# Decoder layer on Trainium2: keys leave PSUM once as f32, and VectorE splits them from SBUF

## What is computed

```python
q = _qdq(x) @ _qdq(wq).T + bq
kv = cond @ wkv.T + bkv
k, v = jnp.split(kv, 2, axis=-1)
...
attn = jax.nn.softmax(jnp.einsum('bnhd,bmhd->bhnm', q, k) * scale, axis=-1)
o = jnp.einsum('bhnm,bmhd->bnhd', attn, v).reshape(B, N, C)
```

## Time and profile before

| what | value |
|---|---|
| runs | 1098.65, 1102.31, 1105.90 us; median 1102.31 |
| profiled execution | 1098.97 us, its span 1097.1 us |
| TensorE busy, whole span | 901.5 us (82%) |
| VectorE busy | 637.3 us (58%) |
| ScalarE busy | 442.1 us (40%) |
| GpSimd busy | 232.9 us (21%) |
| TensorE busy from 410 to 510 us | 89.0 of 100 us, granted clock 0.98 |
| VectorE, ScalarE, GpSimd in the same stretch | 69.3, 49.9, 23.7 us |

### The profile page before, as it was taken

One profiled execution on the slowest core, in us unless ns is written; L12 is line 12 of the kernel. 1 busy time (PEld: TensorE's weight loads), 2 busy tenths in 40 slices (PEclk: granted clock), 3 DMA queues, 4 the chain that ended last, 5 costly groups with the idle time before them and its releaser, 6 DMA issues.

```text
span 1097.1 us, 29125 instructions
## 1 busy us (share of the span) xinstructions
PE 901.5 (82%) x11868; PEld 687.0 (63%) x11869; DVE 637.3 (58%) x1132; ACT 442.1 (40%) x934; POOL 232.9 (21%) x200
## 2 busy tenths in 40 slices
PE   5669988997999899899989988998985059999970
PEld 3547766775777667667766776677763026666750
DVE  5557656765867586767667666866664212323225
ACT  2235444553455454445545554545453012222210
POOL 5123123112212131321123122213000510000016
PEclk9989999998999999999999999999898579999995
DMA  6634342443443343424434343434213783333323
GB/s 208 215 95 129 104 127 82 124 118 90 119 123 107 113 123 100 133 82 118 124 99 120 119 131 91 120 96 128 85 50 142 295 319 121 105 124 110 115 72 100
DMA packets 87696, 136.54 MB, mean 124 GB/s; under 512 B 11522, under 2 KB 75010, under 8 KB 85536
## 3 DMA queue, kind: packets, MB, share of 16 engines
q1 hardware_dynamic: 85040, 123.34, 36.5%
q0 software_dynamic: 2544, 11.54, 2.9%
HBM read 101.66 MB, written 33.10 MB: 123 GB/s over the span
## 4 chain that ended last, share of the span: by engine, by line
PE 53%; issue 13%; DVE 11%; DMA 10%; ACT 7%; POOL 3%; SPq 2%; DVEq 0%; ACTq 0%; POOLq 0%
PE ps L1226 10%; PE ps L1219 8%; PE ps L1506 7%; PE ps L1488 6%; PE ps L1238 5%; DMA k_dram<-k_two 4%; PE ps L1263 4%; ACT k_two L1047 4%; PE ps L1192 4%; DVE k_two L408 3%; DMA k_st<-k_dram 2%; PE ps L1283 2%; ACT pT L1073 2%; PE ps L1303 2%; PE ps L1292 2%
## 5 line engine op out<-in xcount | busy, mean ns | idle before, releaser
L414 DVE TENSOR_REDUCE negmax<-ps 112x1 f32<-112x1500 f32 x128 | 219.9, 1718 | 77.6 <-PE ps L1238 77.5
L1073 ACT ACTIVATE pT<-ps 125x448 f32<-125x448 f32 x384 | 195.0, 542 | 169.1 <-PE ps L1263 168.9
L917 POOL TENSOR_TENSOR ctx_lo<-ctx_raw,ctx_hi 128x1000 fp32r<-128x1000 f32 x47 | 109.1, 2321 | 234.0 <-DVE ctx_hi L400 232.7
L408 DVE SCALAR_TENSOR_TENSOR k_two<-ps,bk_sb,k_two 128x500 f16<-128x500 f32 x96 | 70.7, 736 | 120.1 <-ACT k_two L1047 120.0
L1263 PE MATMUL ps<-qbd,k_st 98*128 98x112 f16 x1536 | 121.7, 216 | 8.5 <-issue 4.0
L1263 PEld LDWEIGHTS ps<-qbd,k_st 98*128 98x128 f16 x1536 | 88.8, 100 | 63.3 <-issue 38.3
L1238 PE MATMUL ps<-k_st,qbd 96*112 96x500 f16 x384 | 108.1, 390 | 15.1 <-DMA k_st<-k_dram 15.1
L1047 ACT ACTIVATE k_two<-ps,bk_sb 128x500 f16<-128x500 f32 x96 | 65.1, 678 | 120.2 <-PE ps L1219 120.2
L1226 PE MATMUL ps<-wkv_hi,ctx_hi 128*125 128x256 f32 x384 | 85.5, 304 | 24.0 <-DVE k_two L408 23.7
L1283 PE MATMUL ps<-pT,v_sb 125*17 125x56 f32 x6144 | 101.4, 215 | 0.5 <-issue 0.5
L1031 ACT COPY v_sb<-ps 125x512 f32<-125x512 f32 x96 | 56.4, 587 | 85.2 <-PE ps L1226 85.2
(11 more groups left out here) (197 smaller groups left out, 1278.4 us busy)
## 6 DMA issues: line engine op xcount, KB each, us to landing
k_st<-k_dram SPq DMA_DIRECT2D x288, 125.0 KB, 2.6
ctx_raw<-ctx_T SPq DMA_DIRECT2D x48, 500.0 KB, 4.1
k_dram<-k_two SPq DMA_DIRECT2D x96, 250.0 KB, 2.4
b_row<-b SPq DMA_DIRECT2D x21, 512.0 KB
w_sb<-w SPq DMA_DIRECT2D x9, 1024.0 KB, 10.8
w_sb<-w POOLq DMA_DIRECT2D x7, 1024.0 KB, 7.4
xs<-zeros SPq DMA_DIRECT2D x1, 2688.0 KB, 9.1
b_row<-b SPq DMA_DIRECT2D x21, 128.0 KB
```

The source lines that it names most:

```text
L408: V.scalar_tensor_tensor(k_two[:, g, 1], ps[:, BANK_KV, 0:MC], bk_sb[:, g:g + 1], k_two[:, g, 0], ALU.add, ALU.subtract).then_inc(unit_out, 1)
L414: V.tensor_reduce(negmax[0:QW], ps[0:QW, BANK_S:BANK_S + CHUNKS, 0:MC], AX.XY, ALU.max, negate=True).then_inc(max_done, 1)
L917: nc.gpsimd.tensor_tensor(ctx_lo[:, k], ctx_raw[:, k], ctx_hi[:, k].bitcast(F32), ALU.subtract).then_inc(ctx_lo_done, 1)
L1073: nc.scalar.activation(pT[0:MT, p % 2, TPC * g:TPC * g + TPC], ps[0:MT, BANK_T + n % 2, 0:TPC * QW].rearrange("p (t n) -> p t n", t=TPC), ...
```

## The change

There is a new f32 tile k_raw in SBUF. ScalarE (now `k_raw_step`) writes the biased keys of a unit into it from the bank and counts `unit_out` itself. VectorE waits for that count, and for the reads of the chunk before (`k_in`), for which ScalarE waited until now; it casts k_raw into the rounded part and subtracts that part from k_raw for the remainder, counting a new semaphore `k_lo_done`, on which SyncE's write to DRAM now waits. ScalarE waits on `k_lo_done` of the chunk before, ahead of overwriting k_raw. All 96 key units change, 6 per batch.

```diff
--- before.py
+++ after.py
@@ -138,6 +138,7 @@
         a_pT = a_kbd[:, 0].rearrange("p c h s -> p (c h s)").rearrange("p (r n) -> p r n", r=PAIRS)
         ctx_hi = sb("ctx_hi", [P, 2, CH, MC], F32R)
         ctx_lo = sb("ctx_lo", [P, 2, CH, MC], F32R)
+        k_raw = sb("k_raw", [P, CH, MC])
         k_two = sb("k_two", [P, CH, 2, MC], F16)
         k_st = sb("k_st", [KA, 2, PAIRS, M + 4], F16)
         q_st = sb("q_st", [KS, PAIRS, P], F16)
@@ -226,6 +227,7 @@
         ctx_lo_done = sem("ctx_lo_done")
         unit_done = sem("unit_done")
         k_hi_done = sem("k_hi_done")
+        k_lo_done = sem("k_lo_done")
         unit_out = sem("unit_out")
         s_done = sem("s_done")
         max_done = sem("max_done")
@@ -402,11 +404,12 @@
             def unit_step(b, par, u):
                 c, g = u // 4, ORDER[u // 4][u % 4]
                 if g < 2:
-                    dve.wait_ge(unit_done, UNITS * b + u + 1)
-
+                    dve.wait_ge(unit_out, UNITS * b + u + 1)
+                    if not (isinstance(b, int) and b == 0 and c == 0):
+                        dve.wait_ge(k_in[g], 48 * (CHUNKS * b + c))
+                    V.tensor_copy(k_two[:, g, 0], k_raw[:, g]).then_inc(k_hi_done, 1)
                     dve.wait_ge(k_hi_done, 2 * (CHUNKS * b + c) + g + 1)
-                    V.scalar_tensor_tensor(k_two[:, g, 1], ps[:, BANK_KV, 0:MC], bk_sb[:, g:g + 1], k_two[:, g, 0],
-                                           ALU.add, ALU.subtract).then_inc(unit_out, 1)
+                    V.tensor_tensor(k_two[:, g, 1], k_raw[:, g], k_two[:, g, 0], ALU.subtract).then_inc(k_lo_done, 1)
 
             def max_step(b, p):
                 n = PAIRS * b + p + 1
@@ -801,7 +804,7 @@
             def k_chunk(b, par, c, ctx_next):
 
                 for g in range(CH):
-                    sp.wait_ge(unit_out, UNITS * b + 4 * c + ORDER[c].index(g) + 1)
+                    sp.wait_ge(k_lo_done, 2 * (CHUNKS * b + c) + g + 1)
                     sp.dma_start(k_dram[g], k_two[:, g]).then_inc(k_out[g], 16)
                     sp.wait_ge(k_out[g], 16 * (CHUNKS * b + c + 1))
                     for i, part in enumerate((0, 1, 0)):
@@ -1037,15 +1040,14 @@
                 act.wait_ge(set_pe, 2 * n + 3)
                 copy((swq_b, swp_b)[n][:], ps[:, BANK_T + n, 0:D]).then_inc(set_act, 1)
 
-            def k_hi_step(b, u):
+            def k_raw_step(b, u):
 
                 c, g = u // 4, ORDER[u // 4][u % 4]
                 if not (isinstance(b, int) and b == 0 and c == 0):
-
-                    act.wait_ge(k_in[g], 48 * (CHUNKS * b + c))
+                    act.wait_ge(k_lo_done, 2 * (CHUNKS * b + c - 1) + g + 1)
                 act.wait_ge(unit_done, UNITS * b + u + 1)
-                nc.scalar.activation(k_two[:, g, 0], ps[:, BANK_KV, 0:MC], ACT.Identity,
-                                     bias=bk_sb[:, g:g + 1]).then_inc(k_hi_done, 1)
+                nc.scalar.activation(k_raw[:, g], ps[:, BANK_KV, 0:MC], ACT.Identity, bias=bk_sb[:, g:g + 1])\
+                    .then_inc(unit_out, 1)
 
             def v_step(b, par, u):
 
@@ -1058,7 +1060,7 @@
             def units(b_next, par, us):
                 for u in us:
                     if ORDER[u // 4][u % 4] < 2:
-                        k_hi_step(b_next, u)
+                        k_raw_step(b_next, u)
                     else:
                         v_step(b_next, par, u)
```

## The result

The changed kernel took a median of 1123.72 us (four runs, 1118.67 to 1130.60), the kernel before, run beside it on the same chip, 1100.71 us: a ratio of 1.0206, interval 1.0137 to 1.0275. Its profiled execution is the fastest of the four, 1118.67 us, and stands against 1098.97: 19.7 us more, where the sum had 15.2. The median lies in the range, 8 us above the forecast.

What follows compares the result with a forecast made beforehand. TensorE, busy 89 of every 100 us of attention, was taken as the bound, with its waits deciding. Terms -12.3 + 11.5 + 8.1 + 5.9 + 2.0 made +15.2 us; forecast 1116 us, range 1094 to 1128.

Steps and rivals of the forecast that it cites:

- A: Projection bank freed earlier by ScalarE, so TensorE's waits on VectorE's remainder go, mostly in slot 1: -12.3 us.
- B: Slot 3 of a pair's first batch: GpSimd's ctx_lo blocks VectorE's cast, delaying nm_row and the shift row: +11.5 us.
- C: Slot 3 of a pair's second batch: ctx_lo blocks the cast, a_xq and TensorE's transposes come later: +8.1 us.
- D: Batch boundaries: keys reach k_st through DRAM later, 15 times 0.39 us: +5.9 us.
- E: Setup and end: first key unit blocked by ctx_lo, small gain in the last projecting batch: +2.0 us.
- The rival: Clock rival: after idling at two places per pair TensorE's matmuls run slower, +17 us more, 1130 us; chance 0.07.
- the first rival: Slot 3: GpSimd hardly blocks VectorE, so second batches lose only 0.39 us each; 1093 to 1096 us; chance 0.30.
- The lock hardly bites: Slot 3 and setup: GpSimd hardly blocks the new operations, sum -7 us, 1093 to 1096 us; chance 0.30 with halfway cases.
- Only the bank counts: Attention stage: VectorE has slack and most of TensorE's 29.0 us of remainder waits goes, 1079 to 1086 us; chance 0.08.

Runs made afterwards that it cites:

- e7: Changed kernel with GpSimd's colliding ctx_lo held until after the key unit, in the setup too; 1087.30 us, 0.9883 of the kernel before.
- e10: The changed kernel again, unaltered, timed as base for the run with filler matmuls; 1121.43 us, 1.0197 of the kernel before.
- e8: Kernel before with an added VectorE cast of a constant SBUF tile behind each key unit, awaited by nobody; 1114.22 us, ratio 1.014.
- e9: Changed kernel with ten dummy matmuls in TensorE's idle time at the end of slot 4, first batches of six pairs; 1113.80 us, ratio 1.0108.
- e11: The changed kernel with both holds on ctx_lo (attention stage and setup), run once more; 1088.25 us, 0.9885 of the kernel before.
- e2: Changed kernel with one GpSimd wait holding the third chunk's ctx_lo until after the key unit, setup not held; 1087.86 us, ratio 0.9896.
- e5: Changed kernel with GpSimd's ctx_lo cut to one column everywhere but in the setup; 1082.20 us, 0.9853 of the kernel before.
- e1: Kernel before with VectorE's remainder reading a constant f32 SBUF tile in place of the projection bank; 1127.14 us, ratio 1.0222.

## Why the prediction was right, and where its terms were off

The ledger compares, slot by slot, when TensorE starts the shift row in the changed kernel's and in the old profile, so it adds up to the profiled difference of the attention stage (last shift row at 852.22 against 832.58, +19.6; the experts behind it take the same time).

The last column is the changed kernel's term less e7's.

| term | predicted | measured | of which the lock, by e7 |
|---|---|---|---|
| A, the bank | -12.3 | -12.7 | |
| B, first batches | +11.5 | +9.2 | +12.9 |
| C, second batches | +8.1 | +6.8 | +5.9 |
| D, keys' way to k_st | +5.9 | +1.9 | |
| E, setup | +2.5 | +4.3 | +3.7 |
| E, the last two batches | -0.5 | -1.9 | |
| slot 7, first batches | 0 | +1.9 | |
| clock, behind B and C | 0 | +13.7 | +13.7 |
| clock, batch 14, slot 2 | 0 | -3.5 | |

**The frame.** The direction, the mechanism and the prices of both new operations were right (0.42 and 0.68 us). The estimate of 0.32 us beside them used only the table of the Trainium skill (VectorE: DVE Perf Modes, section on the TRN2 errata); the note under that table says that its 58 cycles are too few and gives some 150 as measured, by which the estimate would have been 0.42 us, as measured here. Without the clock the terms make 9.5 us where 15.2 were forecast, and the clock adds 10.2 net. The total came near because these two errors go against each other; that is luck.

**A was right in size, but the largest single gain was missed.** The step of a second batch's slot 1 is 0.83 to 0.88 us shorter, seven times, as the 0.84 said; the 0.2 given back to the rotary products is 0.22. The last wait, 2.05 us in the earlier trace rows, was taken as 1.9. It gave 2.28 and then 3.50 more in the next slot, since TensorE had been at the lower clock behind it. The 32 sel_sb matmuls of that next slot, before and after:

```profile
769.40 3.17 PE L1292 MATMUL ps<-sel_sb,oT_sb 128*56 128x17 f32 x32
...
793.36 1.83 PE L1294 MATMUL ps<-sel_sb,oT_sb 128*56 128x17 f32 x32
```

The term that was mis-sized is "about 1.9 of the 2.05": a wait's price ended for me where the wait ends. (In a pair's first batch this gain and the boundary fall in one step; I count 0.86 there.)

**B was right per pair (1.53 us measured, 1.57 worked out), wrong in the first pair and incomplete.** In the first pair the cast began 0.05 us ahead of GpSimd's last mask product and came through. The subtraction was blocked for only 0.7 us, by that product, and ctx_lo behind it waited for the subtraction (2.77 us instead of 2.3):

```profile
91.73 1.27 POOL L928 TENSOR_TENSOR a_kbd<-a_qkT,hmask 128x512 f32<-128x512 f32 x1
...
92.14 1.40 DVE L412 TENSOR_TENSOR k_two<-k_raw,k_two 128x500 f16<-128x500 f32 x1
...
92.97 2.77 POOL L920 TENSOR_TENSOR ctx_lo<-ctx_raw,ctx_hi 128x1000 fp32r<-128x1000 f32 x1
```

Nothing arrived at TensorE, 0 instead of 2.1: in the kernel before, nm_row had been ready at 91.37 us and the shift row began only at 92.18, 0.8 later, and that slack took up the delay. The lock goes both ways: whoever comes second waits. In e7, without ctx_lo in the way, slot 4 of the other six pairs is 0.61 us shorter than before, close to the -0.5 of the prediction, so the lock's own price is 2.14 us per pair.

**The clock was the term left out of the sum.** The rival had it: 1.2 us at 14 places, with a chance of 0.07. The rows give 1.6 at the six places of B (once 2.7) and about 1.5 at two of the seven of C, 13.7 us. Against it I had held that after 1.84 us idle the scores ran at the usual pace. But by my own sum the idle time at B is not 2 us: the 0.42 before the shift row, the 0.75 of the wait that disappears and the 1.57 make 2.74, next to the 2.99 that I had as the example of a costly one. The failing step is "TensorE now idles some 2 us at the two places": I took the idle times of B and C together. At 2.9 us the price came at 11 of 12 places (the changed kernel and e10), at the 1.22 of e8's row not. In C's places, at some 0.8, it came in two of seven batches of the changed kernel and in four of e10's.

**C was right in mechanism, 0.2 us too dear.** The row in the new kernel, and what TensorE shows there:

```profile
346.53 2.31 POOL L920 TENSOR_TENSOR ctx_lo<-ctx_raw,ctx_hi 128x1000 fp32r<-128x1000 f32 x1 [1.19 <-DVE ctx_hi L402]
...
347.88 1.24 DVE L410 CAST k_two<-k_raw 128x500 f16<-128x500 f32 x1 [1.36 <-issue]
...
353.67 0.29 PE L1194 MATMUL ps<-id,a_xq 128*128 128x128 bf16 x2 [0.82 <-DVE a_xq L506]
```

The cast takes 1.24, 0.82 more than alone, which with the 0.39 makes the 1.2 on VectorE; at TensorE 0.14 + 0.79 = 0.93 per batch arrive, in two steps (the 0.82 idle time in the last row is the larger). With the hold of e7 it is 0.9 us over the seven batches, 0.13 each instead of the 0.39 of the first rival.

**D was too large, and I can't size it well.** The boundaries lost 1.9 us in the changed kernel's profile, but by the same reckoning -0.7 in e10's, 1.3 in e9's, and 5.9 and 3.1 in e7's and e11's, whose key path is the same. The sum of the two waits on DMA is 32.8 us in the changed kernel, 31.1 in the earlier trace rows, 37.1 in e7 and 33.5 in e11, the same kernel as e7. So 5.9 is the upper end of what is seen. That each boundary "gets the 0.39" can't be read off these profiles, since the waits on the reads from DRAM vary by more than that between two executions of one kernel; what makes them vary stays open. The term holds clock as well. At the boundary of batch 8 the old profile has the token wait of 2.99 us and the four matmuls of 3.13 behind it; in the new one the slot before is 3.1 us longer (a longer wait for the keys, and matmuls at the lower clock behind it), no token wait was left, and the same four ran at the higher clock, so that slot 1 took 5.8 us less:

```profile
482.90 1.88 PE L1305 MATMUL ps<-wqkv_sb,a_xT 128*128 128x512 f32 x4
```

**E, setup.** The lock costs 3.7 us of it (e7 has 0.6 left), more than the 2.0 taken from the first unit. There the subtraction, not the cast, was blocked, for 2.69 us,

```profile
14.57 0.42 DVE L410 CAST k_two<-k_raw 128x500 f16<-128x500 f32 x1
14.70 2.48 POOL L920 TENSOR_TENSOR ctx_lo<-ctx_raw,ctx_hi 128x1000 fp32r<-128x1000 f32 x1 [8.47 <-DVE ctx_hi L402]
15.02 2.69 DVE L412 TENSOR_TENSOR k_two<-k_raw,k_two 128x500 f16<-128x500 f32 x1
...
19.03 1.13 PE L1310 MATMUL ps<-wqkv_sb,a_xT 128*128 128x256 f32 x4 [2.78 <-DVE a_t L448]
```

and the clock again takes part: granted 0.88 from 0 to 62 us, 0.96 before the change and in e7. Slot 7 of a first batch loses 0.31 us in every kernel with a longer key unit, e7 and e8 among them, and the shift row of slot 8 comes that much later: one more place where TensorE stands behind VectorE's list, which I overlooked.

**The rivals.** *The lock hardly bites* had -7 (by its own sum 1092 to 1095, where it says 1093 to 1096); e2, e5 and e7 are that kernel, and it gives -10 to -13. It lost because GpSimd's work did keep its place: in all six pairs the cast starts 0.11 us behind ctx_lo. *Only the bank counts* had 1079 to 1086, 13 to 20 us less; e7 comes close to the nearer end of it, but with 9.0 us of waits on nm_row left, so VectorE has no slack to spare. The Trainium skill's rule (SBUF — State Buffer, section Who interferes with whom), that operations of VectorE with two SBUF inputs and fast one-tile copies can't run beside GpSimd while one with a single SBUF input outside those fast modes can, is borne out by e1 (0.740 to 2.77 us) and by the two operations of e8 side by side.

**The better kernel.** e7 beats both: 1087.3 and, again, 1088.25 us, 0.9883 and 0.9885 of the kernel before.

## What to carry to other kernels

Taking an operand from PSUM into SBUF can free a bank and at the same time make a VectorE operation collide with GpSimd; before such a change read, at each place, which GpSimd instruction runs beside it and who waits behind VectorE there, and afterwards look at the longest and not the median duration of a line. Work of GpSimd with slack can be held back by one wait on a semaphore that exists already, and should be, once VectorE needs the time. Price a TensorE wait with the rows behind it, not only with its own length, whether you add it or take it away.

## What the runs showed of the hardware that I had not expected

- TensorE's idle time of 2.87 to 2.89 us ahead of the shift row of slot 5 in a first batch was followed by a stretch at 1.2 GHz at all six places in the changed kernel and at five of six in e10, 1.6 us each, but 2.7 to 2.9 once in the one and three times in the other. 2.44 us of dummy matmuls inside the idle time kept the clock at 2.4 GHz.
- Shorter idle times were followed by such a stretch only sometimes, and at other places in another execution of the same kernel: in a second batch's slot 5, with idle times of 0.8, twice in the changed kernel and four times in e10. One of them (355 to 360 us, TensorE busy throughout), with the same matmuls at 0.63 and, 3.8 us later, at 0.40:

```profile
355.00:360.00 5.00, 5.00 (x75) 4.58 (x75) 1.63 (x4) 2.09 (x6) 0.00 (x0) 0.70 0.40 145
...
355.21 0.63 PE L1228 MATMUL ps<-wkv_hi,ctx_hi 128*125 128x256 f32 x2
...
359.00 0.40 PE L1228 MATMUL ps<-wkv_hi,ctx_hi 128*125 128x256 f32 x2
```

  In e11 TensorE was at 1.2 GHz at the end of the last batch (granted 0.50 from 810 to 826 us), in e7, the same kernel, it wasn't (1.00 from 805 to 821 us); the batch took 6.4 us longer for it. So the clock moves a kernel's time by several us between executions.
- The block shows only as duration. No row of the waits names ctx_lo as what a VectorE instruction waited for; the 18.5 us are found by the mean of a group against its median.
